# A second buffer for one weight block, and two blocks' low halves made by GpSimd, in an FFN kernel of seven-product multiplications

## What is computed

```python
def cond(x, weight, bias, lora_a, lora_b, scaling, adapter_id):      # cut
    base = jnp.einsum('bsi,oi->bso', x, weight) + bias
    low = jnp.einsum('bsi,bri->bsr', x, lora_a[adapter_id])
    delta = jnp.einsum('bsr,bor->bso', low, lora_b[adapter_id])
    return base + scaling[adapter_id][:, None, None] * delta

w = (NF4[codes.reshape(-1)].reshape(-1, 64) * absmax[:, None]).reshape(codes.shape)
out = x + jnp.einsum('bsd,od->bso', cond(x, ...), w) + bias2          # x: (8, 512, 2048)
```

## Time and profile before

| | us |
|---|---|
| median of 3 runs (2129.02 to 2129.52) | 2129.19 |
| the profiled execution | 2133.57 |
| its span, from first to last instruction | 2131.4 |
| TensorE busy | 2023.9 (95%) |
| VectorE busy | 1601.4 (75%) |
| ScalarE busy | 884.4 (41%) |
| GpSimd busy | 44.6 (2%) |
| DMA | 526.14 MB, 247 GB/s over the span |

### The profile page before, as it was taken

One profiled execution on the slowest core, in us unless ns is written; L12 is line 12 of the kernel. 1 busy time (PEld: TensorE's weight loads), 2 busy tenths in 40 slices (PEclk: granted clock), 3 DMA queues, 4 the chain that ended last, 5 costly groups with the idle time before them and its releaser, 6 DMA issues.

```text
span 2131.4 us, 29421 instructions
## 1 busy us (share of the span) xinstructions
PE 2023.9 (95%) x10880; PEld 1719.1 (81%) x10880; DVE 1601.4 (75%) x2401; ACT 884.4 (41%) x1417; POOL 44.6 (2%) x55
## 2 busy tenths in 40 slices
PE   3899999999999999999989989989998998998997
PEld 3788778788878787889979989979986886886876
DVE  8999879867986465566577677786777777777887
ACT  7755555555555232343442242252242234224332
POOL 4100000000000000000000000000000000000000
PEclk8999999999999999999999999999999999998999
DMA  9778888887887889755577678677786877867876
GB/s 278 241 239 263 252 253 256 250 269 247 260 262 240 260 252 297 246 189 186 198 243 255 213 273 263 209 264 227 260 276 214 273 241 237 263 215 246 270 265 230
DMA packets 406277, 526.14 MB, mean 247 GB/s; under 512 B 22992, under 2 KB 293024, under 8 KB 406008
## 3 DMA queue, kind: packets, MB, share of 16 engines
q1 hardware_dynamic: 402824, 513.23, 75.0%
q0 software_dynamic: 3312, 11.03, 1.6%
HBM read 336.47 MB, written 188.76 MB: 246 GB/s over the span
## 4 chain that ended last, share of the span: by engine, by line
PE 86%; DVE 5%; DMA 4%; issue 2%; SPq 2%; ACT 2%; DVEq 0%; ACTq 0%
PE big L1605 20%; PE big L1607 20%; PE big L1606 20%; PE big L1793 10%; PE big L1791 9%; PE big L1620 2%; DVE comb L1291 1%; DMA a_br<-a_sel_d 1%; DMA xg<-xc_d 1%; PE big L1601 1%; ACT wq_nat_w L904 1%; DMA code_w<-in_L_ffn_codes_dram 1%; DMA comb_raw<-wc_d 1%; SPq L544 1%; PE big L1797 0%
## 5 line engine op out<-in xcount | busy, mean ns | idle before, releaser
L1791 PE MATMUL big<-comb,xs 128*128 128x256 f32 x1920 | 474.8, 284 | 25.7 <-DVE comb L1291 12.5
L1793 PE MATMUL big<-comb,xs 128*128 128x272 f32 (+1 forms) x1920 | 473.4, 288 | 0.0
L1605 PE MATMUL big<-wq,tile 128*128 128x512 f32 x1088 | 468.0, 430 | 1.1 <-DVE tile L1226 1.0
L1607 PE MATMUL big<-wq,tile 128*128 128x512 f32 x1088 | 426.8, 392 | 0.0
L1606 PE MATMUL big<-wq,tile 128*128 128x512 f32 x1088 | 425.8, 391 | 0.0
L1605 PE MATMUL big<-comb,xs 128*128 128x512 f32 x928 | 371.9, 401 | 28.0 <-DVE comb L1291 15.5
L1791 PEld LDWEIGHTS big<-comb,xs 128*128 128x128 f32 x1920 | 367.8, 192 | 31.8 <-DVE comb L1291 26.9
L1793 PEld LDWEIGHTS big<-comb,xs 128*128 128x128 f32 x1920 | 368.0, 192 | 2.3
L1606 PE MATMUL big<-comb,xs 128*128 128x512 f32 x928 | 369.6, 398 | 0.0
L1607 PE MATMUL big<-comb,xs 128*128 128x512 f32 x928 | 368.9, 398 | 0.0
L1419 DVE TENSOR_TENSOR r_sb<-big,r_sb 128x512 f32<-128x512 f32 x328 | 225.7, 688 | 168.3 <-PE big L1607 112.7
(11 more groups left out here) (135 smaller groups left out, 2159.7 us busy)
## 6 DMA issues: line engine op xcount, KB each, us to landing
raw<-in_L_cond_weight_dram SPq DMA_DIRECT2D x128, 512.0 KB, 4.6
xg<-xc_d SPq DMA_DIRECT2D x112, 512.0 KB, 5.3
xc_d<-rq SPq DMA_DIRECT2D x26, 1792.0 KB, 7.7
r_sb<-m_d SPq DMA_DIRECT2D x80, 512.0 KB, 5.0
m_d<-r_sb SPq DMA_DIRECT2D x64, 512.0 KB, 6.1
wc_d<-cs SPq DMA_DIRECT2D x31, 896.0 KB, 4.9
tb<-wc_d SPq DMA_DIRECT2D x107, 256.0 KB, 4.8
x_nat<-in_x_dram SPq DMA_DIRECT2D x104, 256.0 KB, 4.0
```

Source lines behind the costliest of these rows:

```text
L1605: nc.tensor.matmul(out_ap, t_hi, m_hi, start=first, stop=False, skip_group_check=onto)
L1607: return nc.tensor.matmul(out_ap, t_lo, m_hi, start=False, stop=last, skip_group_check=onto)
L1791: nc.tensor.matmul(big[:, bank, 0:HW], x, w[:, 0:HW], start=begin, stop=end, skip_group_check=not opens)
L1793: ins = nc.tensor.matmul(big[:, bank + 1, 0:wide], x, w[:, HW:HW + wide], start=begin, stop=end, skip_group_check=not opens)
```

## The change

SS1's block gets a second place, `comb_ss1_odd` at 160 KB, used by odd passes. The four places `tb`, in which sums are made, lie there too, so they get a second set, at 33 KB where SS1's first place is; a pass's sums are made in the set that lies in the place that its own SS1 will take. SS1 is loaded in unit q = 6, ScalarE copies it behind product 4 of that unit, and VectorE subtracts behind product 6 and behind product 0 of q = 7. Its load waits for the stores of all four sums. `halves_of` counts SS1 first.

For passes 1 to 6 the low halves of A12 and A22 are made by GpSimd, in a loop at the end of its program, each behind ScalarE's copy. They count on a semaphore of their own, `s_clo_p`. In VectorE's table `LO_STEPS` the ten left stand at other products. The load of the totals in the last unit of pass 5 moves from product 1 to product 2 and waits for product 1.

```diff
+    BY_GPSIMD, ON_VECTOR = (A12, A22), 10
...
     def halves_of(i):
         if i:
-            return [(f, c) for f in INNER for c in range(2)]
+            return [(f, c) for f in (SS1, A11, S2, S4, S3, A12, A22) for c in range(2)]
...
-    LO_STEPS = {2: [0], 3: [1], 4: [2, 3], 5: [4], 6: [5, 6], 7: [7], 8: [8, 9], 9: [10], 10: [11, 12], 11: [13]}
+    LO_STEPS = {-1: [0], 0: [1], 2: [2], 3: [3], 5: [4], 6: [5, 6], 7: [7, 8], 8: [9]}
...
-        if q == QB - 1 and i < LAST and k >= 2:
+        if q == QB - 2 and i < LAST and k == 4:
+            return [(i + 1, SS1)]
+        if q == QB - 1 and i < LAST and k >= 2 and k != 3:
             return [(i + 1, INNER[k - 2])]
...
+        cw2 = [cw[SS1], at("comb_ss1_odd", 160, [P, QT, 2, SW], F32R)]
+        cr2 = [cr[SS1], at("comb_raw_ss1_odd", 160, [P, QT, 2, SW], F32)]
+
+        def comb(i, f):
+            return cw2[i % 2] if f == SS1 else cw[f]
...
-        tb = [at(f"tb{i}", 160 + 4 * i, [P, HALF, SW], F32) for i in range(4)]
+        tb = [[at(f"tb{m}_{i}", kb + 4 * i, [P, HALF, SW], F32) for i in range(4)] for m, kb in enumerate((33, 160))]
...
-            return tb_late[n] if (i, c) == (0, 1) and n < B22 else tb[n]
+            return tb_late[n] if (i, c) == (0, 1) and n < B22 else tb[1 if i == 0 else i % 2][n]
...
+                    if f == SS1:
+                        for n in range(4):
+                            sp.wait_ge(s_wist[n], 16 * stored(n, i + 1, 0))
+                    else:
+                        sp.wait_ge(s_wist[KIND_OF[f]], 16 * (stored(KIND_OF[f], i, c) + 1))
...
-                    if turn:
+                    if q == QB - 2 and i < LAST and k == 1:
+                        for c in range(2):
+                            load_half_comb(i + 1, SS1, c)
+                    if turn and k != 1:
                         sp.wait_ge(s_prod, NF * u + k + 1)
...
-                    if k == 1 and u + 1 == BOTH:
+                    if k == 2 and u + 1 == BOTH:
+                        sp.wait_ge(s_prod, NF * u + 2)
                         for m in range(2):
                             load_total(BOTH, m)
...
+            for i in range(1, NF):
+                for n in range(ON_VECTOR, 2 * NF):
+                    f, c = halves_of(i)[n]
+                    ks = slice(HALF * c, HALF * (c + 1))
+                    pool.wait_ge(s_chi, 2 * NF * i + n + 1)
+                    tt(cw[f][:, ks, LO, 0:SW], cr[f][:, ks, LO, 0:SW], cw[f][:, ks, HI, 0:SW].bitcast(F32),
+                       ALU.subtract).then_inc(s_clo_p, 1)
...
-                    pe.wait_ge(s_clo, max(half_at(i, f, c) for c in range(2)))
+                    pe.wait_ge(s_clo_p if i and f in BY_GPSIMD else s_clo, max(half_at(i, f, c) for c in range(2)))
```

More of the change, by code:

```diff
@@ L216, in half_at @@
     def half_at(i, f, c):
-        return 2 * NF * i + halves_of(i).index((f, c)) + 1
+        n = halves_of(i).index((f, c)) + 1
+        if i and f in BY_GPSIMD:
+            return 4 * (i - 1) + n - ON_VECTOR
+        return 2 * NF + ON_VECTOR * (i - 1) + n if i else n
     def stored(n, i, c):
@@ L235, in adaln_ffn_kernel @@
                  for p, k, n in ((0, 0, B11), (0, 1, B12), (0, 6, B22), (1, 0, B21))}
-    LO_STEPS = {2: [0], 3: [1], 4: [2, 3], 5: [4], 6: [5, 6], 7: [7], 8: [8, 9], 9: [10], 10: [11, 12], 11: [13]}
+    LO_STEPS = {-1: [0], 0: [1], 2: [2], 3: [3], 5: [4], 6: [5, 6], 7: [7, 8], 8: [9]}
     def lo_halves(u, k):
         i, q = divmod(u, QB)
-        if q == QB - 1 and i < LAST:
-            return [(i + 1, n) for n in LO_STEPS.get(k, [])]
+        if q >= QB - 2 and i < LAST:
+            return [(i + 1, n) for n in LO_STEPS.get(k - NF * (QB - 1 - q), [])]
         if q == 0 and i:
@@ L300, in adaln_ffn_kernel, with comb_raw @@
             cr.append(at(f"comb_raw{f}", cw_kb[f], [P, QT, 2, wide], F32))
+        cw2 = [cw[SS1], at("comb_ss1_odd", 160, [P, QT, 2, SW], F32R)]
+        cr2 = [cr[SS1], at("comb_raw_ss1_odd", 160, [P, QT, 2, SW], F32)]
+        def comb(i, f):
+            return cw2[i % 2] if f == SS1 else cw[f]
+        def comb_raw(i, f):
+            return cr2[i % 2] if f == SS1 else cr[f]
         xs_kb = {A11: 184, SS1: 188, S2: 192, S4: 105, S3: 109, A12: 113, A22: 117}
@@ L393, in adaln_ffn_kernel @@
         s_ident = sem("identity_rounded")
+        s_clo_p = sem("block_low_by_gpsimd")
         s_wa = sem("last_a11_weights_stored")
@@ L536, in store_sum @@
                 sp.wait_ge(s_ws, sum_at(i, c, n))
-                sp.dma_start(wi_d[i, n, c], tb[n][:, :, :].rearrange("p k o -> p (k o)")).then_inc(s_wist[n], 16)
+                sp.dma_start(wi_d[i, n, c], block_at(i, c, n)[:, :, :].rearrange("p k o -> p (k o)")).then_inc(s_wist[n], 16)
             def load_half_comb(i, f, c):
@@ L543, in load_half_comb @@
                     for jj in range(2):
-                        sp.dma_start(cr[f][:, HALF * c:HALF * (c + 1), LO, jj * HW:(jj + 1) * HW],
+                        sp.dma_start(comb_raw(i, f)[:, HALF * c:HALF * (c + 1), LO, jj * HW:(jj + 1) * HW],
                                      wc_d[2 * half + jj, OUTER[i], :, ks, :]).then_inc(s_cld[f][c], 16)
                 else:
-                    sp.wait_ge(s_wist[KIND_OF[f]], 16 * (stored(KIND_OF[f], i, c) + 1))
-                    sp.dma_start(cr[f][:, HALF * c:HALF * (c + 1), LO, 0:SW],
+                    if f == SS1:
[3 more added lines that the diff above has]
+                        sp.wait_ge(s_wist[KIND_OF[f]], 16 * (stored(KIND_OF[f], i, c) + 1))
+                    sp.dma_start(comb_raw(i, f)[:, HALF * c:HALF * (c + 1), LO, 0:SW],
                                  wi_d[i, KIND_OF[f], c].rearrange("p (k o) -> p k o", k=HALF)).then_inc(s_cld[f][c], 16)
@@ L559, in load_last_b22 @@
                     for lo, hi in ks[jj]:
-                        sp.dma_start(tb[B22][:, lo - QT - HALF:hi - QT - HALF, jj * HW:(jj + 1) * HW],
+                        sp.dma_start(tb[1][B22][:, lo - QT - HALF:hi - QT - HALF, jj * HW:(jj + 1) * HW],
                                      wc_d[2 + jj, OUTER[0], :, lo:hi, :]).then_inc(s_wl[B22], 16)
@@ L966, in comb_hi @@
                     act.wait_ge(s_cld[f][c], half_bytes(i, f, c))
-                    src = cr[f][:, ks, LO, 0:SW]
-                nc.scalar.copy(cw[f][:, ks, HI, 0:SW], src).then_inc(s_chi, 1)
+                    src = comb_raw(i, f)[:, ks, LO, 0:SW]
+                nc.scalar.copy(comb(i, f)[:, ks, HI, 0:SW], src).then_inc(s_chi, 1)
             def x_hi(u, f):
@@ L1289, in comb_lo @@
                 else:
-                    src = cr[f][:, ks, LO, 0:SW]
-                tt(cw[f][:, ks, LO, 0:SW], src, cw[f][:, ks, HI, 0:SW].bitcast(F32),
+                    src = comb_raw(i, f)[:, ks, LO, 0:SW]
+                tt(comb(i, f)[:, ks, LO, 0:SW], src, comb(i, f)[:, ks, HI, 0:SW].bitcast(F32),
                    ALU.subtract).then_inc(s_clo, 1)
@@ L1782, in multiply @@
                     x_hi, x_lo = x_slot(u, f)[:, HI, kt, :], x_slot(u, f)[:, LO, kt, :]
-                    w_hi, w_lo = cw[f][:, kt, HI, :], cw[f][:, kt, LO, :]
+                    w_hi, w_lo = comb(i, f)[:, kt, HI, :], comb(i, f)[:, kt, LO, :]
                     first, last = opens and kt == 0, kt == QT - 1
```

## The result

| | before | after |
|---|---|---|
| median of 4 runs, us | 2129.36 (2129.02 to 2136.93) | 2107.78 (2105.49 to 2110.11) |
| profiled execution, us | 2133.57 | 2105.49 |
| its span, us | 2131.4 | 2103.7 |

The ratio is 0.989, with a 95% interval of 0.9876 to 0.9904: the kernel is faster by 1.1%. (Every ratio here is that of the mean times to those of the kernel before in the same set of runs; kernels of different sets are best compared by it.) The forecast was 2111.4, in a range of 2083 to 2143.

The account below looks back on a forecast made before the run. TensorE, busy 95% of the span, was taken to bound the kernel, losing 67.7 us in six turns. Gains of 2.0, 1.7, 3.7, 3.3, 3.1 and 4.0 made 17.8 us: median 2129.19 to 2111.4, range 2083 to 2143.

Parts of the forecast that it names:

- the turns: First units of a pass, product 0 to the next unit's product 0, six (T1 to T6); claimed to lose 67.7 us.
- The wait before product 2: TensorE in each turn: SS1 earlier removes it, but for 0.5 us left in T3 and 2.1 in T6.
- The step that failed: In the turns, 1.05 MB fewer loads ahead bring each later transfer 2.9 us forward, taken off waits after T1.
- The hold: In the turns, each GpSimd subtraction stops VectorE's two-input SBUF instructions for 2.62 us, alternating; additions of products pass.
- The step by step sum: Queues followed through the six turns: 2.0, 1.7, 3.7, 3.3, 3.1 and 4.0 us won, 17.8 in all.
- part 1: SS1's block gets its own place for odd passes, work done a unit earlier: over 20 us won alone.
- part 2: A12's and A22's splits on GpSimd: VectorE loses 4.6 us a turn but is held; gives back some gain.
- The clock: TensorE, after a wait of over 2 us: granted 1.2 instead of 2.4 GHz, priced at 1.6 us a wait.
- the change wouldn't act: Rival: product 2 still waits, because of ScalarE behind S2's load; about 2127 us; chance 0.12, shared with a slightly longer hold.
- Splits held in a row: Rival: GpSimd's splits follow without a gap in the turns, VectorE gets nothing between; +7 us, 2136.5; chance 0.12.
- longer ones: Rival: a GpSimd split takes 5.2 us, turns grow by 6 to 8 us, +40 in all, 2169; chance 0.11.
- hidden: Rival: GpSimd's splits fall on VectorE's idle time and additions in the turns; 57 us won, 2072; chance 0.20.

Follow-up runs that it names:

- second profile of the changed kernel: The changed kernel measured again without any edit, in the next set of runs: 2107.09 us, ratio 0.9875 to the kernel before.

## Why the prediction held, and where not

**What bounds the kernel: right.** What was won, 25.3 us, was won in the turns. The label of T6 was wrong by one product (above); 70.5 us were to be won.

**The number: nearer than its working.** The medians moved by 21.6 us, 17.8 were forecast. The turns won 25.3, and the profiled executions differ by 28.1. So the sum was too small by 7.5 us in the turns, and part of the closeness of 2107.78 to 2111.4 comes from the two profiled executions lying off their medians in opposite directions. That is luck.

**The wait before product 2: right in five turns, wrong in T6.** It is gone in T1 and T5 and 0.30, 0.58 and 0.60 us in T2 to T4; 0.5 was forecast for T3. (In the second profile of the changed kernel 1.29 us are left in T1, where VectorE first waited 1.71 us for ScalarE's x.) In T6 2.1 us should have remained of 5.07, and 4.60 did. The step that failed took 2.9 us of earlier transfers off the wait. That sum was made from SS1's 1.05 MB in the turn. In T6 ScalarE waited 4.08 us for S4's first half all the same, and the copy of product 0 began 9.6 us into the turn in place of 10.1, 0.5 earlier and not 2.9. S3's loads, which it stands behind, were issued at 1910.64, 1.0 us into the turn, where before they were at 1935.83, 1.6 into it. In SyncE's queue they stand behind the loads of g. (The first row is of after, the second of before.)

```profile
1910.64 1.23 SPq L569 DMA_DIRECT2D comb_raw<-wi_d  x2
1935.83 1.23 SPq L548 DMA_DIRECT2D comb_raw<-wi_d  x2
```

T6 won 3.1 us (35.15 to 32.04) in place of 4.0.

**The hold: right in kind, too large in size.** GpSimd and VectorE alternate once both are at work, no row of VectorE is long enough for two of GpSimd's splits, and the additions go through. The forecast price was 2.62 us for each GpSimd split; VectorE was held for 1.56 on average. The 2.62 came from a row of VectorE that began 0.37 us ahead of GpSimd's and whose hold, so counted, was longer than GpSimd's whole instruction (2.38 us, to 58.44, which is after the 58.31 of the text); the earlier trace rows bear 2.38 at most. In T1 its rows were held for 1.77, 2.15 and 1.57, since an instruction that comes while GpSimd is already at work stands only for the rest of it, and GpSimd's first split fell into the 2.08 us in which VectorE was waiting for a transfer. GpSimd's own splits were said to last 2.4 us, or up to 3.6; they last 2.34, and up to 4.31.

**The step by step sum: right in direction, 7.5 us too small.**

| | T1 | T2 | T3 | T4 | T5 | T6 | won |
|---|---|---|---|---|---|---|---|
| before, us | 29.75 | 29.87 | 32.65 | 33.17 | 32.51 | 35.15 | |
| forecast | 27.7 | 28.2 | 28.9 | 29.9 | 29.4 | 28.4 | 17.8 |
| after | 26.61 | 27.33 | 28.54 | 27.49 | 25.82 | 32.04 | 25.3 |

The forecast of T6 started from 32.36, hence 28.4; from 35.15 the same step gives 31.2. In T1 the waits were to be 2.1 us before product 3 and 3.7 before product 4, in all 5.8; there was one of 4.95 before product 4. GpSimd's first split began 6.0 us after the turn did, forecast were 5.7. But S4's second split and S3's first ran at 1070.50 in 2.35 us, unheld, and GpSimd's first was the one to stand, so the addition of product 1 began 7.6 us into the turn (1072.77), not 10.2 (1078.4). T4 and T5 lost much less than forecast: 3.11 and 0.36 us of waits in T5, not 2.0 and 4.6. The 4.6 before product 6 is the term that was oversized most; that the price of the hold made it so is likely, but was not worked through. The new waits are released by r_sb, as forecast, and stand before products 3, 4 and 6, but not all in each turn: before product 4 alone in T1 and T2, before 3 and 4 in T3 and T4. The prediction doesn't name the wait of 2.10 us that T1 had before product 4 already.

**"Of it part 1 would give over 20 alone, and part 2 gives some of it back": wrong.** The buffer alone gave 0.83%, about 18 us, and GpSimd added 6 us by the medians (2113.24 and 2107.1) and up to 9 by the ratios (0.9917 and 0.9875). As far as its text shows, the step costed GpSimd's splits by what VectorE's queue becomes shorter (4.6 us) against what it is held. It didn't count, for the buffer alone, what they no longer stand behind: the work on x in all turns, and the 2.85 to 6.41 us in which VectorE waits for x in T4 to T6. These are the waits before product 5, 26.4 us. The rows for it stood there: the wait of 3.55 us for xg in the earlier trace rows, and the wait on comb of up to 5.7 us in the earlier trace rows. The text even said that the splits stood behind that transfer, but used it in the sums of T5 and T4 alone, and not for the kernel with the buffer only.

**The clock: right in T1.** Behind the wait of 4.95 us in T1 the window of TensorE after shows the lower level for part of the stretch:

```profile
1082.00:1086.00 4.00, 4.00 (x24) 0.65 0.45 169
```

T1's mean clock is 0.94, and 0.06 x 26.61 = 1.6 us, the price that was taken.

**Rivals.** That the change wouldn't act fell with the waits before product 2; of T6 it was nearly true. Splits held in a row didn't come, nor did longer ones: uncontended they take 2.34 us, as long as the row of another subtraction promised. Had they been hidden, 2072 was the figure. With GpSimd only writing, and in 0.96 us each, 2077.09 was measured: the price was near, and that is not what happened.

## What to carry to other kernels

When an instruction stands late, look first at what is ahead of it in its own queue: an instruction that waits for a transfer, or work that nobody waits for yet. Putting the urgent work in front gave 21 to 24 us here, on top of the second buffer and without another engine, where the move to a second engine gave 6 to 9. GpSimd paid here by having a queue of its own, and it cost, as both engines read SBUF with two-input instructions, 1.56 us of VectorE and 0.70 of GpSimd for each subtraction; price such a move by the instructions that stand between a wait and its release, not by VectorE's busy share. And a wait that is removed can come back further on if the next instruction stands behind the same thing: twice here in T6, behind the same transfers, and in T1, behind GpSimd's hold.
